# A DLRM tower on one core: one unrolled list of steps, eleven lookups per block, paired one-hots and feature-major embeddings

## The reference

```python
e = jnp.stack([tbl_0[ids[:, 0]], ..., tbl_25[ids[:, 25]]], axis=1)          # (2048, 26, 128)
combined = jnp.concatenate([dense[:, None, :], e], axis=1)                   # (2048, 27, 128)
interactions = jnp.einsum('bfd,bgd->bfg', combined, combined)
iu, ju = jnp.triu_indices(27, k=1)
z = jnp.concatenate([dense, interactions[:, iu, ju]], axis=1)                # 128 + 351
h = jnp.concatenate([z, dense], axis=1)                                      # 607
h = jnp.maximum(h @ W_top1 + b_top1, 0.0)                                    # 512
h = jnp.maximum(h @ W_top2 + b_top2, 0.0)                                    # 256
y = h @ W_top3                                                               # (2048, 1)
```

## Time and profile before

| What | us |
|---|---|
| median of three runs | 431.82 |
| lowest and highest run | 426.78, 437.46 |
| span of the profiled execution | 432.4 |
| TensorE busy | 330.4 |
| GpSimd busy | 308.9 |
| VectorE busy | 239.1 |
| ScalarE busy | 179.4 |

### The profile page before, as it was taken

One profiled execution on the slowest core, in us unless ns is written; L12 is line 12 of the kernel. 1 busy time (PEld: TensorE's weight loads), 2 busy tenths in 40 slices (PEclk: granted clock), 3 DMA queues, 4 the chain that ended last, 5 costly groups with the idle time before them and its releaser, 6 DMA issues.

```text
span 432.4 us, 13310 instructions
## 1 busy us (share of the span) xinstructions
PE 330.4 (76%) x5360; PEld 266.8 (62%) x5360; DVE 239.1 (55%) x471; ACT 179.4 (41%) x363; POOL 308.9 (71%) x280
## 2 busy tenths in 40 slices
PE   0785719677699998286879999376969999867596
PEld 0563517466578876275668877264758887656475
DVE  2776625397569563266768664075666758023531
ACT  2144223720746546220546545420564546323442
POOL 6887878887778877777778878777777877772000
PEclk9899977888979999659969999666879999986699
DMA  5467853435435345426444543526354442221000
GB/s 155 153 177 191 239 167 109 128 92 151 115 110 149 118 122 117 133 52 167 119 130 114 158 116 106 141 55 169 77 172 100 142 123 71 55 57 28 5 0 0
DMA packets 24707, 49.51 MB, mean 115 GB/s; under 512 B 8010, under 2 KB 10586, under 8 KB 24653
## 3 DMA queue, kind: packets, MB, share of 16 engines
q1 hardware_dynamic: 15916, 30.83, 22.4%
q0 software_dynamic: 8704, 17.84, 17.5%
q10 hardware_dynamic: 32, 0.01, 0.0%
HBM read 48.65 MB, written 0.01 MB: 113 GB/s over the span
## 4 chain that ended last, share of the span: by engine, by line
PE 65%; issue 15%; DMA 10%; ACT 5%; DVE 3%; SPq 0%; ACTq 0%; DVEq 0%
PE mix_ps L454 12%; PE emb_ps L436 12%; PE emb_ps L438 11%; PE emb_ps L416 6%; DMA lookup_ids<-ids_looked_up 5%; DMA table<-table 5%; PE mlp_ps L485 4%; PE mlp_ps L488 4%; PE mlp_ps L486 4%; PE mlp_ps L436 3%; PE mlp_ps L438 3%; DVE one_hot L650 2%; ACT emb L535 2%; PE mlp_ps L498 2%; PE mlp_ps L501 2%
## 5 line engine op out<-in xcount | busy, mean ns | idle before, releaser
L396 POOL DMA_INDIRECT rows<-table,gather_ids x272 | 307.9, 1132 | 83.6 <-issue 81.7
L650 DVE TENSOR_SCALAR one_hot<-lookup_ids,row_number 125x512 fp32r<-125x512 int32 x288 | 124.8, 490 | 43.6 <-DMA lookup_ids<-ids_looked_up 17.6
L436 PE MATMUL emb_ps<-one_hot,table_h 125*128 125x512 f32 x224 | 94.2, 421 | 19.1 <-DVE table_l L640 18.7
L454 PE MATMUL mix_ps<-emb 128*26 128x26 f32 x4096 | 57.7, 202 | 54.3 <-issue 51.5
L438 PE MATMUL emb_ps<-one_hot,table_l 125*128 125x512 f32 x224 | 91.9, 410 | 0.0
L454 PEld LDWEIGHTS mix_ps<-emb 128*26 128x26 f32 x4096 | 49.5, 115 | 63.6 <-issue 61.7
L543 ACT ACTIVATE table_h<-table 125x1024 fp32r<-125x1024 f32 x36 | 38.0, 1060 | 88.9 <-DMA table<-table 52.4
L535 ACT ACTIVATE emb<-emb_ps 128x512 f32<-128x512 f32 (+1 forms) x80 | 46.9, 651 | 56.5 <-PE emb_ps L416 53.2
L663 DVE COPY gram<-mix_ps 128x416 f32<-128x416 f32 x32 | 27.8, 874 | 74.3 <-PE mix_ps L454 74.1
L436 PEld LDWEIGHTS emb_ps<-one_hot,table_h 125*128 125x128 f32 x224 | 44.6, 199 | 31.7 <-ACT emb L535 12.1
L549 ACT ACTIVATE emb<-emb_ps 128x512 f32<-128x512 f32 x28 | 34.0, 1215 | 50.2 <-PE emb_ps L438 50.1
(11 more groups left out here) (50 smaller groups left out, 278.4 us busy)
## 6 DMA issues: line engine op xcount, KB each, us to landing
table<-table SPq DMA_DIRECT2D x36, 500.0 KB
lookup_ids<-ids_looked_up SPq DMA_DIRECT2D x36, 256.0 KB, 5.4
rows<-table,gather_ids POOLq DMA_INDIRECT x272, 3.9
dense_rows<-dense SPq DMA_DIRECT2D x4, 256.0 KB, 4.1
gram<-w_pairs SPq DMA_DIRECT2D x2, 256.0 KB
gram<-w_dense SPq DMA_DIRECT2D x2, 256.0 KB
h_full<-w SPq DMA_DIRECT2D x1, 512.0 KB
gather_ids<-ids_gathered SPq DMA_DIRECT2D x16, 8.5 KB, 10.2
```

The source lines that it names most:

```text
L396: pool.indirect_dma_start(out=rows[:, t, g, :], out_offset=None, in_=tables[GATHERED[g]], in_offset=bass.IndirectOffsetOnAxis(ap=gather_id ...
L436: pe.matmul(bank[:, :], table_h[0:TROWS, i % 2, cols], hot, start=(c == 0), stop=False)
L454: last = pe.matmul(bank[32 * j:32 * j + SIDE, SIDE * q:SIDE * q + SIDE], emb[:, s, 1:FEATURES], emb[:, s, 0:SIDE], start=True, stop=True)
L650: dve.tensor_scalar(one_hot[0:TROWS, hot_slot(i, c), :], lookup_ids[0:TROWS, i % 2, :], row_number[0:TROWS, c:c + 1], None, ALU.is_equal) \
```

## The change

One list STEPS, made by giving every step a time in units of blocks and sorting, takes the place of BODY, TAIL and the loops; every engine runs through it once. In it:

- Eleven tables are looked up, fifteen gathered. `rows` holds two tiles; a group's gathers wait for the transposes of the same group two tiles back. There are four embed steps per tile, the last one with the dense features.
- The tables are padded on the host to 1024 rows and loaded as 128 partitions of 8 rows. In the first two blocks they are split as before; in block 1 each split table (high and low, 1 MB) is also written to a scratch tensor in HBM ("spill"), and in blocks 2 and 3 it is read from there, with no split.
- Ids come as int16; ScalarE writes a second copy less one, and one VectorE instruction of 2 x 512 elements makes two chunks' one-hots. Four such pairs are one lookup's and the only buffers.
- `emb` is feature-major: [feature, 128 samples] per tile, ten tile places with overlap. Copies write neighbouring elements; the Gram matmuls read their 26 features 128 elements apart.
- Gram matrices stand in half steps of 32 matmuls between half lookups of 8 matmuls. A tile's matrices start when all lookups of its block are in place.
- Pairs are cut in bands for two tiles at once, ten ScalarE copies, in another order of rows; `w1_pairs` is ordered alike on the host. Layers run in units of 4, 4, 4, 2 and 2 tiles. The unsplit Relu of layer 1 is written back to PSUM. `mix_ps` has two banks, `mlp_ps` three.
- GpSimd's descriptor scratch is given as 8192 bytes.

```diff
-LOOKUPS = 9
+LOOKUPS = 11
...
+    def look_time(k, h):
+        b, i = divmod(k, LOOKUPS)
+        return b - 1 + (i + h / 2 + (0.3 if b > 0 else 0.0)) / LOOKUPS
+
+    for k in range(LOOKS):
+        at(look_time(k - 3, 1) if k >= 3 else -2.0 + k / 10, "load", k)
+        at(look_time(k - 2, 1) + 0.002 if k >= 2 else -1.9 + k / 10, "less", k)
+        if k < SPLIT_BLOCKS * LOOKUPS:
+            at(look_time(k - 1, 0) - 0.001 if k >= 1 else -1.5, "split", k)
+        if SPLIT_BLOCKS - 1 == k // LOOKUPS and SPLIT_BLOCKS < BLOCKS:
+            at(look_time(k, 0) - 0.002, "spill", k)
+        for h in range(2):
+            at(look_time(k - 1, h) + 0.001 if k >= 1 else -1.4 + h / 10, "hots", k, h)
+            at(look_time(k, h), "look", k, h)
+    for t in range(TILES):
+        at((t - 4) / PER_BLOCK + 0.01 if t >= 4 else -1.95 + t / 10, "drow", t)
+        for e in range(EMBEDS):
+            at((t + 0.02 + 0.06 * e) / PER_BLOCK if t > 0 else (-0.6, -0.5, -0.4, -0.3)[e], "embed", t, e)
+        for n in (2 * t, 2 * t + 1):
+            for h in range(2):
+                at((t + 0.4 + 0.3 * (n % 2) + 0.14 * h) / PER_BLOCK, "gram", n, h)
+        if t % 2 == 1:
+            at((t + 1.1) / PER_BLOCK, "pairs", t // 2)
...
+    STEPS = [step for _, _, step in sorted(timed)]
...
+            def load(k):
+                i, s = k % LOOKUPS, k % HL
+                if is_split(k):
+                    wait(sp, table_low, k - RAW + 1)
+                    sp.dma_start(raw[:, k % RAW, :],
+                                 tables[LOOKED_UP[i]].rearrange("(p c) d -> p (c d)", c=CHUNKS)) \
+                        .then_inc(raw_in[k % RAW], 16)
+                else:
+                    wait(sp, hot_used, QUADS * (k - HL + 1))
+                    j = (SPLIT_BLOCKS - 1) * LOOKUPS + i
+                    sp.wait_ge(spilled[j % HL], 16 * spills(j))
+                    if is_split(k - HL):
+                        sp.wait_ge(spilled[s], 16 * spills(k - HL))
+                    sp.dma_start(table_hl[:, s, :, :].bitcast(fp32), scratch[i]).then_inc(hl_in[s], 16)
...
+            def spill(k):
+                sp.wait_ge(table_low, k + 1)
+                sp.dma_start(scratch[k % LOOKUPS], table_hl[:, k % HL, :, :].bitcast(fp32)).then_inc(spilled[k % HL], 16)
...
+                for e in range(EMBEDS):
+                    wait(pool, embeds_done, EMBEDS * (t - ROWS) + e + 1)
...
+            def less(k):
+                act.wait_ge(lids_in[k % LIDS], 16 * (k // LIDS + 1))
+                act.activation(lids[:, k % LIDS, 1, :], lids[:, k % LIDS, 0, :], ACT.Copy, bias=-1.0) \
+                    .then_inc(less_one, 1)
+
+            def split(k):
+                act.wait_ge(raw_in[k % RAW], 16 * (k // RAW + 1))
+                wait(act, hot_used, QUADS * (k - HL + 1))
+                if spills(k - HL) > 0:
+                    act.wait_ge(spilled[k % HL], 16 * spills(k - HL))
...
+                for p in (2 * h, 2 * h + 1):
+                    wait(dve, hot_used, QUADS * (k - 1) + p + 1)
+                    dve.tensor_scalar(hot[:, p, :, :], lids[:, k % LIDS, :, :],
+                                      row_number[:, 2 * p:2 * p + 1], None, ALU.is_equal).then_inc(hot_ready, 1)
...
                     last = pe.matmul(bank[32 * j:32 * j + SIDE, SIDE * q:SIDE * q + SIDE],
-                                     emb[:, s, 1:FEATURES], emb[:, s, 0:SIDE], start=True, stop=True)
+                                     emb[:, f + 1:f + FEATURES, s], emb[:, f:f + SIDE, s], start=True, stop=True)
```

More of the change, by code:

```diff
@@ L67, in dlrm_tower @@
+    WIDE = 14
+    PLACE = [1, 2, 3, 4, 5, 6, 7, 8, 1, 2, 3, 9, 4, 5, 6, 7]
+    PLACES = 10
     HALF = 16
-    GRAMS = TILE // 4 // HALF * TILES
     KCH = [128, 128, PAIRS - 256, DIM]
     N1, N2 = HIDDEN1 // 128, HIDDEN2 // 128
[L71 to L114, removed]
-        [("layer2", n) for n in range(N2)] + [("layer3",), ("none",)]
@@ new lines, in features, with places @@
+        def features(tile):
+            return WIDE * (PLACES - 1 - PLACE[tile])
+        def places(b, f):
+            tiles = range(b * PER_BLOCK, (b + 1) * PER_BLOCK)
+            even = all(PLACE[t] == PLACE[t - 1] + 1 for t in tiles[1:])
+            for run in ([tiles] if even else [tiles[:-1], tiles[-1:]]):
+                first = (features(run[0]) + f) * TILE
+                pitch = (PLACES * WIDE - 1) * TILE
+                yield (slice((run[0] - tiles[0]) * TILE, (run[-1] + 1 - tiles[0]) * TILE),
+                       bass.AP(emb, first, [[pitch, 128], [-WIDE * TILE, len(run)], [1, TILE]]))
@@ new lines, in dense_part, with is_split, reloads, spills @@
+        def dense_part(dense_x, tile):
+            return dense_x[:, tile // PER_BLOCK % 2, (tile % PER_BLOCK) * TILE:(tile % PER_BLOCK + 1) * TILE]
+        def is_split(k):
+            return k < SPLIT_BLOCKS * LOOKUPS
+        def reloads(k):
+            return len([j for j in range(k % HL, k + 1, HL) if not is_split(j)])
+        def spills(k):
+            return len([j for j in range(k % HL, k + 1, HL) if is_split(j) and j >= (SPLIT_BLOCKS - 1) * LOOKUPS])
+        def unit_cols(u):
+            return slice(0, TILE * UNITS[u][1])
@@ L378, in _ @@
+            sp.dma_start(gather_ids[:, 0, :], ids_gathered[:, 0, :]).then_inc(first_ids_in, 16)
+            run({"load": load, "spill": spill, "drow": drow, "weights": weights})
         @block.gpsimd
@@ new lines, in gram @@
+            def gram(n, h):
+                tile, side = n // 2, n % 2
+                bank = mix_ps[n % 2]
+                if h == 0:
+                    if side == 0:
+                        b = tile // PER_BLOCK
+                        pe.wait_ge(emb_placed, max([placed["look", k, 1] for k in range(b * LOOKUPS, (b + 1) * LOOKUPS)] +
+                                                   [placed["embed", tile, e] for e in range(EMBEDS)]))
+                    wait(pe, gram_out, n - 1)
+                for q in range(h * HALF // 2, (h + 1) * HALF // 2):
```

863 lines of the change are left out of this document (409 added, 454 removed).

## The result

The changed kernel takes 449.88 us (median of four runs, 449.38 to 450.42); beside it the kernel before took 430.84 us. The ratio is 1.0455, with a 95% interval of 1.0374 to 1.0536: slower, where 390 us was forecast and 428 us was the top of the range.

A forecast was written before the change was run, and what follows sets the result against it. Two floors on each other, GpSimd's gathers (393 us) and TensorE with its issue gaps, bound the kernel. Last tile transposed at 357, plus 10 to the last Gram matmul, plus 22 tail: 389, said as 390 us; own range 372 to 405, full 372 to 428.

The forecast's parts named there:

- Reading across samples' stride: Gram matmuls on TensorE reading operands 512 bytes apart: 29, 7 or 0 ns more each; taken as nothing.
- rival 1: Strided Gram reads bind TensorE: at 29 ns more per matmul, 30 us per block, 475 us in all; chance 0.11.
- The turning point: Extra price per strided Gram matmul from which the kernel becomes over 2% slower: about 20 ns.
- Prologue: First block's lookups: 4.3 us each, tile 1's transposes at 73 us, GpSimd waiting 5.5 us.
- Tables under 4 us: Sign that the forecast is right: table loads take under 4 us, where one took 8.64 us before.
- one-hots at 0.76 us: VectorE's double one-hot instructions: 0.76 us each, 176 of them; 1.21 us if at TENSOR_TENSOR's rate.
- the issue gaps before Gram matmuls close: TensorE's issue waits vanish through interleaved lookups, under 10 us in all; otherwise 15 us per block return.
- tail 22 us: From the last Gram matmul to the end: 22 us, where it was 25.6 us.
- no split that waits for a spill: ScalarE's split waits for the spill three lookups back, with about 20 us left; nothing taken.
- nothing taken for GpSimd's descriptor scratch: GpSimd's newly set scratch: no cost taken; 34 us more if every gather had to wait.
- the gathers' floor: GpSimd never stops issuing its 272 gathers until about 393 us, so speeding TensorE alone gives nothing.
- Spills: Table writes to HBM on SP, with later loads queued behind: nothing taken; 15 us if a spill took 25 us.

The follow-up runs named there:

- e5: Changed kernel with only the Gram matmuls' stationary operand (weight load) reading neighbouring elements, the moving one still strided; 415.92 us, one run.
- e6: Changed kernel with only the Gram matmuls' moving operand reading neighbouring elements, the stationary one still strided; 420.75 us, one run.
- e18: Changed kernel, emb still feature-major (strided Gram reads), with weights split later, four id buffers and ids issued ahead of tables; 431.13 us, ratio 0.9971 to before.
- e8: Changed kernel with emb sample-major, weights split later, four id buffers and ids issued ahead of tables; 391.4 us, ratio 0.9058 to before.
- e1: Changed kernel with emb turned back to sample-major, so Gram operands are neighbours again, nothing else; 407.56 us, ratio 0.9376 to before.
- e16: Kernel before with tables padded to 1024 rows and loaded in 128 rows of partitions instead of 125; 433.71 us, ratio 1.0015.

## Why the prediction was wrong, point by point

**The step that failed** is "Reading across samples' stride ... I take nothing". Its bracket was right (0, 7 or 29 ns per Gram matmul; measured 14.0), its choice was not. The reason given, that four strips run side by side and so hide the reads, fails: one strided operand alone costs 5.3 to 5.7 ns (e5, e6). 4096 x 14.0 ns are 57 us more of TensorE's time; the kernel's time rises by 39.7 us (e18 against e8). It was rival 1 that came true, with a chance of 0.11 and at half its price. The nearest row, stood on its side (1.1 ns per element more on ScalarE) and I argued it away. By rival 1's own price, 85 us at 29 ns, the middle of the bracket would have been about 42 us more: 432 us and no gain.

**What no step held:** the strided reads slow the other engines. A gather takes 1266 instead of 1042 ns between e18 and e8, a double one-hot 1026 instead of 756, and ScalarE's split of the first layer's result (line 572) 1254 instead of 602. I had sized rival 1 by TensorE alone, and the slower gathers are on the path (25% of e18's chain).

**The turning point,** slower by over 2%, I put at 20 ns per matmul; rival 1's price (85 us at 29 ns) makes it 17. At 14 ns and with the waits of weights and ids mended the kernel stands level with before (e18), so 14 ns cancels the gain already. The 18.8 us of waits then make it slower at a price below 20 ns.

**Prologue: mechanism right, two terms mis-sized.** A lookup takes 4.8 us, not 4.3, because ids land 4 us after their slot is freed; over fourteen lookups that is 7 us. The weights' wait of 13.1 us on ScalarE had no term at all: the forecast named what stands behind a spill on SP, and not what stands on ScalarE and VectorE behind the last of nine loads. Together 20 of the 22.7 us by which tile 1 is late (95.7 instead of 73). "Tables under 4 us" was wrong (median 5.3 us) and did no harm.

**Right:** one-hots at 0.76 us (shortest, median and longest 672, 751, 3536 ns in the changed kernel; the mean of 999 there falls to 753 without the strides, e1); the issue gaps before Gram matmuls close (2.9 us idle; in e1 3.1 us on issue; in e8, which waits less elsewhere, 13.4, above the 10 that I had set); tail 22 us (427.9 to 448.4, 20.5); no split that waits for a spill; nothing taken for GpSimd's descriptor scratch (a gather's median is 947 ns in e8 as in the earlier trace rows); the gathers' floor, shown by e16.

**Spills, right only in part.** No split waited for one, but SP did: 17.7 us in the changed kernel, for three spills, before the reloads that need them. There it is not on the chain that ended last; in e1 two spills are, with 12.7 us, and ids stand behind them. The forecast named this queue and took nothing for it.

**The rest of the sum.** In e8, where the strides and the weights' wait are taken out and most of the ids' wait, it comes true place by place, within 5.2 us. Starts of the first transposing matmul of a tile, and the last gather, in us:

| | forecast | after | e18 | e8 |
|---|---|---|---|---|
| tile 1 | 73 | 95.7 | 77.5 | 78.2 |
| tile 4 | 138 | 155.8 | 139.8 | 141.3 |
| tile 8 | 226 | 260.0 | 237.8 | 227.3 |
| tile 12 | 314 | 358.2 | 335.7 | 311.5 |
| last gather ends | 352 | 410.0 | 391.8 | 353.7 |
| time | 390 | 449.9 | 431.1 | 391.4 |

A middle block takes 86.0 and 84.2 us in e8 (forecast 88), 98 us in e18. The agreement at the gathers is partly luck: they were to cost 345 us with 5.5 us of waiting, and cost 250.2 + 68.9 = 319 us with 31.8 us of it.

**Loads in 128 rows, and strided operands.** The first load in 128 rows of partitions is split from 4.6 us on, in 125 rows from 8.9 us on (e16 against the kernel before). A strided operand costs TensorE 5.3 to 5.7 ns per Gram matmul of 26 elements, and two cost 14.0. The Trainium skill, SBUF — State Buffer, section Door 1: The DMA port swizzle, says that each access that crosses to a new 16-byte line pays a penalty; the trace agrees as far as that goes, and the price is this case's.

## What to carry to other kernels

A change of layout is paid for by the reader that reads most often. When no row shows an engine reading at a stride, take the middle of the bracket, leave at most one operand strided (about 5.5 ns here, where two were 14), and reckon what the reads do to the other engines as well. A gain on one of two engines that bind together is worth nothing until the other moves too (e16: 16 us earlier, no gain). And a mended wait uncovers the next one: without the strides, mending the weights' wait gave 1.6 us, within the noise, and mending weights and ids 16.2.

## What the runs showed of the hardware that was not expected

- TensorE reading both operands of small matmuls at a stride of 512 bytes slows engines that work on other data: beside one burst of 3.23 us a gather took 4.17 us instead of 0.94. With one operand strided the gathers kept their 1034 ns. By what path the engines hinder each other was not tried.
- With short groups of Gram matmuls between long matmuls, the issue gaps before them are 3.1 us (e1) and 13.4 us (e8) instead of 51.5. The loop was unrolled in the same change, and the two were not tried apart.
- One kernel on one chip can take 432 or 700 us in different sittings, with 2.6 us of issue between single short matmuls where it takes 700. Why was not found.
